# Order of work at the entry of a state scan: the second half's projections moved in among the first scan units

## The reference, cut to what matters

```python
x_proj = x @ proj_in_w.T + proj_in_b
delta = jax.nn.softplus(x_proj @ B_w.T)          # 16 step sizes per token
sigA = jax.nn.sigmoid(A)                         # 256 x 16 decays
def step(h, inp):                                # over the 256 tokens of a sequence
    x_t, d_t = inp
    h = h * sigA + x_t[:, :, None] * d_t[:, None, :]
    y_t = h.sum(axis=1) @ C_w.T + D_param * x_t
    return (h, y_t)
```

## Time and profile before

| | |
|---|---|
| median of 3 runs | 715.25 us (710.79, 715.25, 716.66) |
| profiled execution, its time | 715.68 us |
| its span in the trace | 713.6 us |
| mean granted TensorE clock | 0.98 of full speed |
| PE busy | 662.3 us, 93% of the span |
| DVE busy | 467.6 us, 66% |
| ACT busy | 348.5 us, 49% |
| POOL busy | 346.5 us, 49% |

### The profile page before, as it was taken

One profiled execution on the slowest core, in us unless ns is written; L12 is line 12 of the kernel. 1 busy time (PEld: TensorE's weight loads), 2 busy tenths in 40 slices (PEclk: granted clock), 3 DMA queues, 4 the chain that ended last, 5 costly groups with the idle time before them and its releaser, 6 DMA issues.

```text
span 713.6 us, 12706 instructions
## 1 busy us (share of the span) xinstructions
PE 662.3 (93%) x4586; PEld 516.5 (72%) x4586; DVE 467.6 (66%) x1085; ACT 348.5 (49%) x807; POOL 346.5 (49%) x473
## 2 busy tenths in 40 slices
PE   5989989999899898798999999999999999999994
PEld 5856667856457554556788888878769888888884
DVE  4579868463135599998878777752456665566655
ACT  4656536241511774444979898870353222222224
POOL 5326416341101669355778788752344444455521
PEclk9999999999989899899999999999999999999998
DMA  8000007001003000000000000003001121111001
GB/s 278 1 2 2 2 2 294 1 1 49 0 0 84 2 16 0 2 1 1 1 1 2 3 1 2 1 2 111 17 28 49 41 59 53 45 45 45 1 1 59
DMA packets 10351, 23.31 MB, mean 33 GB/s; under 512 B 2033, under 2 KB 5074, under 8 KB 9906
## 3 DMA queue, kind: packets, MB, share of 16 engines
q1 hardware_dynamic: 10002, 22.24, 9.5%
q10 hardware_dynamic: 288, 0.26, 0.1%
HBM read 21.45 MB, written 1.05 MB: 32 GB/s over the span
## 4 chain that ended last, share of the span: by engine, by line
PE 74%; DVE 17%; ACT 4%; issue 3%; POOL 2%; DMA 1%; POOLq 0%; SPq 0%; DVEq 0%; ACTq 0%
PE psum L445 40%; DVE A L1478 6%; PE psum L1068 4%; PE psum L483 4%; PE psum L1081 4%; PE psum L506 4%; PE psum L844 2%; PE psum L557 2%; PE psum L889 2%; PE psum L599 1%; DVE A L1344 1%; DVE x_tok L1224 1%; DVE stats L1217 1%; PE psum L463 1%; PE psum L563 1%
## 5 line engine op out<-in xcount | busy, mean ns | idle before, releaser
L445 PE MATMUL psum<-parts 128*128 128x256 f32 (+2 forms) x1440 | 246.3, 329 | 8.9 <-DVE parts L1298 7.3
L445 PEld LDWEIGHTS psum<-parts 128*128 128x128 f32 (+1 forms) x1440 | 215.6, 191 | 36.5 <-DVE parts L1298 7.3
L2088 POOL TENSOR_SCALAR probs<-probs,row_rec 128x256 f32<-128x256 f32 x128 | 70.8, 565 | 27.4 <-DVE row_rec L1288 24.4
L2002 ACT ACTIVATE A<-psum 128x512 f32<-128x512 f32 x44 | 26.3, 598 | 115.5 <-PE psum L445 115.5
L1478 DVE TENSOR_TENSOR_SCAN A<-decay,psum 128x256 f32<-128x256 f32 x128 | 75.4, 664 | 6.0 <-PE psum L889 6.0
L1584 DVE TENSOR_TENSOR A<-A,psum 128x512 f32<-128x512 f32 x44 | 30.1, 687 | 70.6 <-ACT A L2002 58.4
L1689 ACT ACTIVATE probs<-probs,neg_max 128x256 f32<-128x256 f32 x128 | 63.7, 500 | 17.4 <-DVE neg_max L1279 17.4
L1279 DVE CUSTOM_DVE_ANT_0 probs<-psum,ctxT 128x256 f32<-128x256 f32 x128 | 48.9, 419 | 22.2 <-PE psum L445 20.5
L445 PE MATMUL psum<-parts,A_rounded 128*128 128x256 f32 x372 | 54.8, 283 | 1.6 <-DVE A_rounded L1420 1.6
L2246 POOL CAST parts<-C 128x512 fp32r<-128x512 f32 x22 | 13.5, 611 | 85.3 <-PE psum L445 74.9
L445 PEld LDWEIGHTS psum<-parts,A_rounded 128*128 128x128 f32 x372 | 48.7, 191 | 2.9 <-DVE A_rounded L1420 2.1
(11 more groups left out here) (250 smaller groups left out, 1288.0 us busy)
## 6 DMA issues: line engine op xcount, KB each, us to landing
C<-in_experts SPq DMA_DIRECT2D x22, 384.0 KB, 3.0
A<-in_w_o SPq DMA_DIRECT2D x1, 2048.0 KB, 12.4
x_tok<-in_x_tok SPq DMA_DIRECT2D x1, 1024.0 KB, 7.2
ctxT<-in_ctxT SPq DMA_DIRECT2D x1, 1024.0 KB, 10.6
A<-in_w_uqT SPq DMA_DIRECT2D x1, 768.0 KB, 6.3
out<-x_tok SPq DMA_DIRECT2D x6, 128.0 KB, 1.8
xT<-in_xT SPq DMA_DIRECT2D x2, 256.0 KB, 4.1
C<-in_wqk SPq DMA_DIRECT2D x1, 512.0 KB, 4.4
```

The costliest lines, as they stand in the source:

```text
L445: ins = mm(o, left[l], right[r], start=first and n == 0, stop=last and n == 2, skip_group_check=True)
L2088: last = pool.tensor_scalar(pr, pr, row_rec[:, u % RING[n], j:j + 1], 1.0, ALU.mult, ALU.mult)
```

## The change

PE and ACT get a new order at the scan's entry. ACT's `softplus(0)` stands directly behind `projected(0)`. PE's `ln_transposes(2, 1)` stands behind unit 0's transposes, `in_proj(1)` behind unit 1's, `step_sizes(1)` and `tokens_back(1)` behind unit 2's. On ACT `ln_out(2, 1)` stands behind unit 0's scaling, `projected(1)` behind unit 2's, the copies into `x_p` behind unit 3's, `softplus(1)` behind unit 4's. All pieces of the keys' preparation up to the first half's rotations move one unit later on PE, ACT and POOL. No instruction is added or removed.

```diff
@@ PE
             step_sizes(0)
             pe.wait_ge(sem("s_xpT"), 2)
             tokens_back(0)
-            ln_transposes(2, 1)
-            in_proj(1)
             pe.wait_ge(sem("s_soft"), 1)
             pe.wait_ge(sem("x_p"), 2)
             for n in range(SCAN_UNITS):
@@
+                if n == 0:
+                    ln_transposes(2, 1)
                 if n == 1:
+                    in_proj(1)
+                if n == 2:
                     step_sizes(1)
                     tokens_back(1)
-                if n == 3:
+                if n == 4:
                     loaded(pe, "w_kvc", "w_kr", "w_dq")
                     pe.wait_ge(sem("x_p"), 4)
                     key_latents(0)
-                if n == 4:
+                if n == 5:
                     key_latents(1)
-                if n == 6:
+                if n == 7:
                     latents_by_token()
-                if n == 7:
+                if n == 8:
                     key_ropes(0, 0)
-                if n == 8:
+                if n == 9:
                     key_ropes(0, 1)
@@ ACT
             projected(0)
-            ln_out(2, 1)
             softplus(0)
             for n in range(SCAN_UNITS):
                 scale_tokens(act, n, (0, 1), ...)
-                if n == 1:
+                if n == 0:
+                    ln_out(2, 1)
+                if n == 2:
                     projected(1)
-                if n == 2:
+                if n == 3:
                     for w in range(2):
                         ... # the copies into x_p
-                if n == 3:
+                if n == 4:
                     softplus(1)
-                if n == 4:
+                if n == 5:
                     latents_out(0)
-                if n == 5:
+                if n == 6:
                     latents_out(1)
-                if n == 7:
+                if n == 8:
                     ... # kv_tok
-                if n == 8:
+                if n == 9:
                     ropes_out(0, 0)
-                if n == 9:
+                if n == 10:
                     ropes_out(0, 1)
@@ POOL
-            ROTATE_AT = (10, 11, 12, 13, 19, 20, 21, 22)
+            ROTATE_AT = (11, 12, 13, 14, 19, 20, 21, 22)
```

## The result

| | before | after |
|---|---|---|
| median, measured together (16 runs each) | 712.76 us | 718.38 us (713.59 to 722.74) |
| ratio, 95% interval | | 1.0076 (1.0058 to 1.0094) |
| profiled execution, its time | 715.68 us | 713.59 us |
| its span | 713.6 us | 711.5 us |

The change makes the kernel 0.8% slower, about 5.4 us. The profiled execution of after happens to be the shortest of its 16, and looks faster than that of before. So the two spans can't be compared; the stages can. The first step is a common point. I take the start of `step_sizes(0)` on PE (line 865): up to there the two programs are the same. It lies at 228.04 us before and at 222.43 after.

The account below looks back on a forecast made before the run. DVE was taken to set the pace inside the scan. Its waits of 12.4 us, less 1.5 before and 5.0 from an earlier first scan, gave +5.9 us: 721 us against 715.25, range 712.5 to 724.5.

Parts of the forecast that it names:

- The mark: Start of unit 8 in DVE's scan, 260.1 us before; whatever moves there moves to the end, predicted +5.9 us.
- Softplus and PE's start: Scan's entry: softplus at 230.05, unit 0's transposes at 233.45 instead of 238.97; DVE's first scan gains 5.0 us.
- The Trainium skill's draining: ACT ahead of unit 0's scaling: about 1.38 us per table switch, making scaling 1.4 us later; not counted.
- Low clock at unit 0: PE idles 2.3 us instead of 0.7 ahead of unit 0, so low clock expected there; first scan at 234.65.
- the clock stays low until somewhere in `in_proj(1)`: PE in front of unit 2: clock could rise within in_proj(1), taken as 4.6 us, between 3.7 and 5.54.
- the price of transposes at the low clock: PE's scan transposes: 2.2 us for eight at the low clock, against 1.0 at full clock.
- Units 3 to 7: DVE's waits in front of these units, behind PE work and ACT hand-offs: 1.3, 0, 1.1, 2.4 and 0 us.
- What lies behind unit 8: key_ropes and POOL's rotations, one unit later, stay hidden; otherwise 0.1 to 0.3 us a unit for four units.
- The sum: DVE's waits of 12.4 us, less 1.5 before and 5.0 gained: +5.9 us on 715.68, giving 721.6.
- rival B: Scan's entry, hand-offs at full clock: +1.5 to +3.5 us, 717 to 719; chance 0.22.
- the case I called likeliest: Scan's entry with the clock low to somewhere in in_proj(1): +5.9 us; chance 0.42.
- Rival A: Scan's entry: PE never held back by ACT, DVE's waits under 6.5 us, 711.4 us; chance 0.15.

Follow-up runs that it names:

- Taking the latents apart: Changed kernel with key_latents(1) on PE and latents_out(1) on ACT each one unit later; 1.0057 of the kernel before.
- the spread version: Changed kernel with ln_transposes(2, 1) in PE's wait ahead of unit 0 and later PE, ACT and key pieces drawn apart over the units; 0.9974 of before.
- the second measurement: The changed kernel run again without any edit; 1.0066 of the kernel before.
- the second spare-matmul version: Changed kernel with two spare matmul calls into an unread bank behind tokens_back(0), in PE's wait ahead of unit 0; 1.006 of the kernel before.

## Why the prediction was right, point by point

- **The mark is DVE's.** Right. Behind unit 10 DVE is busy without a gap again, and from `merge(0)` to the end both programs take the same: 428.1 us before (713.6 - 285.54), 428.3 after (711.5 - 283.24), and 428.0 to 428.9 in the other four profiles of the two.
- **Softplus and PE's start.** Right to 0.1 us: first scan 4.91 us earlier, 5.0 predicted.
- **The Trainium skill's draining ("ScalarE: Activation LUTs", section "What ACT_TABLE_LOAD costs").** The trace after doesn't show it either: scaling begins 2.37 us behind the start of softplus.
- **Low clock at unit 0.** Right that it is low, but not for the reason I gave. It fell at 225.35, when PE's wait in front of unit 0 had only begun; in the kernel before it also falls 2.1 to 2.8 us behind `step_sizes(0)`, ahead of the 0.69 us pause that I counted among its causes. Two terms behind it failed. The first is that the clock stays low until somewhere in `in_proj(1)`. After the change it was back at 232.3, before unit 1's transposes, in both profiles: `in_proj(1)` took 3.6 us, not 4.6, and unit 1's transposes 1.1, not 2.2. The second is the price of transposes at the low clock. I took 2.2 us for eight from the earlier trace rows, where they took turns with a DVE that was busy without a gap; here, all at the low clock, unit 0's eight took 1.7 us and `ln_transposes` 1.9. Together unit 1 waited 2.28 us, not 3.6, and unit 2 1.89, not 4.0. Of the 3.4 us between, by the same walk, about 0.8 are the second term and the rest the first.
- **Units 3 to 7.** 1.24, 0, 1.16, 2.22 and 0 us against 1.3, 0, 1.1, 2.4 and 0: the hand-offs were sized right, each at the place that the walk named. Taking the latents apart, and the spread version, confirm the causes by removing them.
- **What lies behind unit 8.** I wrote that `key_ropes` stays hidden, or costs 0.1 to 0.3 us a unit. It cost 0.64 us once, in front of unit 10, where it now meets `state_sums(1)`.
- **The sum.** DVE's waits up to unit 7 were 12.4 in the sum and measured 8.8. The stage moved by 3.3 us, not 5.9, which is my rival B (hand-offs at full clock, +1.5 to +3.5) rather than the case I called likeliest. With the 1.6 us of the low clock taken off it is 1.7, close to the 1.5 that I had for the hand-offs alone.
- **The time.** 721 was forecast and 718.4 measured; as a difference, +5.9 by the sum and about +5.4 by the runs. That agreement is partly luck, because the stage explains only 3.3 of it. The forecast's 2.6 us too many come from its base: 715.25 us from three runs, where the 16 measured together gave 712.76.

The other 2 us are open. The stage's 3.3 us are 1.0046 as a ratio, inside the interval of the second measurement (1.0042 to 1.009) but below that of the first (1.0058 to 1.0094). What the runs show of the rest: sorted by mean granted clock, executions at 0.980 or less have medians of 715.4 us before (25 of 86 executions with a clock on record) and 718.5 after (22 of 26); those above, 712.5 before (61 of 86) and 716.0 after (only 4 of 26). At like clock the change costs 3.1 to 3.6 us, as the stage shows; the rest goes with the change's executions being at the lower mean clock more often, which holds among runs measured together too (8 of 10 against 11 of 35). The profiles of the two kernels show one difference that goes with it: the three with a mean of 0.980 have a low stretch of 7 us at about 192 to 200 us, ahead of the scan, and the three with 0.984 to 0.987 don't. The code there is the same in both kernels, so why the change's executions should have it more often, if that is what they have, no run shows. Whether before runs the entry at full clock in executions that were not profiled, which would give 2.3 us more (55.2 against 57.5), could not be settled: four profiles show no such case.

Rival A (faster) needed DVE's waits under 6.5 us. They were 8.8; the spread version shows what it would have taken.

## What to carry to other kernels

An engine that eats from a ring of two is not fed by starting earlier but by what stands between its feeds: walk the feeder's list unit by unit, with every crossing to another engine, before moving a block into the loop, and put work into a wait that exists anyway (here one block of transposes: 1.9 us of the stage, 4 us by the ratios). Where a later piece moves by one unit, look whether it now meets another in the same unit. And compare stages from a common point, in more than one profile: here equal code ahead of the change differed by 5.6 us between two executions, as much as the whole effect.

## What the runs showed of the hardware

- The low clock is dear and irregular. The same `in_proj(1)` took 3.6 to 5.9 us. In the four profiles of before the clock rose 3.5 to 4.4 us behind its start, at a different point each time, and yet unit 0's transposes followed 10.93 us behind `step_sizes(0)` in all four. In the second spare-matmul version the clock fell although PE had paused for only 0.78 us ahead of the step sizes and gone on without a pause behind them. The Trainium skill ("TensorE: Matmul & The Clock Gate", Part 1) says that the point of change varies between runs of one kernel; the profiles agree.
- A small DVE `tensor_tensor` (128x64) took 1.07 us beside a POOL instruction of 1.27 us, and 0.20 us where POOL was idle. POOL's row of the spread version:

```profile
261.71 1.27 POOL L2159 TENSOR_TENSOR C<-C 128x512 f32<-128x512 f32 x1 [8.30 <-ACT C L1875]
```

  DVE's ran from 261.99 to 263.06, POOL's from 261.71 to 262.98: DVE's came to its end only when POOL's had. The Trainium skill ("SBUF — State Buffer", section "SBUF: two separate sides") states this, an exclusive lock of the shared port for an operation of DVE with two SBUF inputs, and the two runs agree.
